# A windowed-attention and mixture-of-experts layer on one core: the first layer's projections in plain fp32 on 64-row tiles, and new pattern and attention stages

## The chip, the core and the metric

The kernel runs on one NeuronCore of a Trainium2 chip, one launch. The metric is the device time of that core in microseconds, median of the runs shown. It is written in Bass: every engine (TensorE or PE, VectorE or DVE, ScalarE or ACT, GpSimdE or POOL, SyncE or SP for the DMAs) has its own instruction stream, and they are tied together by semaphores by hand.

## What is computed

x is (2, 32, 32, 64), fp32: 2048 tokens of 64 channels, in 32 windows of 8 x 8. The first layer is an attention-like mixer with 8 heads of 32, the second a top-2 mixture of 8 experts.

```python
t = layernorm(x) @ W_prep + b_prep              # 64 -> 5 kinds x 8 heads x 32: q_n, q, k, k_m, v
bias, pat_n, pat_m = spatial(intrinsic)         # relative tables, 15 x 15 offsets
score  = bias + einsum('bhod,ohid->bohi', q_n, pat_n)      # pattern of the query's place
score += einsum('bhod,bhid->bohi', q, k)
score += einsum('bhid,ohid->bohi', k_m, pat_m)             # pattern of the key's place
score  = (score - mean_i) / sqrt(var_i(score) + 1e-5)      # no softmax
x = x + (einsum('bohi,bhid->bohd', score, v)) @ W_fin + b_fin
# second layer, on xt = layernorm(x)
logits = xt @ Wr + br;  two best experts, weights from their probabilities
y_e = gelu((layernorm(xt) * ln_g[e] + ln_b[e]) @ W1[e] + b1[e]) @ W2[e] + b2[e]
x = x + sum of the two chosen y_e, weighted
```

## The kernel before

Everything is kept in SBUF. The work is in four stages; TensorE's order is written out by hand: the early part line by line, `stage_b` (L70) gives the order of the pattern stage, and `pe_steps(t)` (L101) that of attention and FFN, one list for each step t. `make_plan` turns these lists into the fill and drain counts of the eight PSUM banks, and `begin`, `end`, `filled` and `drained` wait and count by them.

**Projections (L524 to L605).** DVE and ACT normalise x twice side by side into XN (token by channel), PE transposes it (L532) into PSUM, and `XS` gets the upper 64 partitions rounded to F32R (ACT, L846) and in the lower 64 the rest (DVE, L1038). W_prep lies twice under itself in `WS`; ACT and POOL split it into `WHI` and `WLO` (L836, L848, L434). `project` (L551) multiplies all 128 rows of XS by WHI and by WLO, two F32R matmuls, and so gets nearly fp32. `prep` (L557) makes the two query kinds and the key pattern kind in chunks c = 0 to 5 of four banks each, `keys` (L547) makes K. `shift_bias` (L514) folds ln_b into the experts' first bias: 16 matmuls with one column each, half ahead of the first projections and half behind the second chunk, from W1E, loaded for it. `centred` (L536) makes the windows' centred values XC. ACT and DVE take the results out of PSUM: `stage` (L796) into `STG`, KT at L863 and L1053, XC at L867 and L1058. SP then copies STG by DMA into `BD` (L368), a buffer that holds for every head only its own 32 rows, the others zero, so that one matmul with all 128 rows keeps four heads apart. There are two BD buffers of 1024 columns for six chunks.

**Pattern stage (`pattern`, L568).** 32 tiles of one bank; in each, for four places u and two head groups g, a matmul of a slice of the tables PN or PM (128 rows, 64 columns) with 128 columns of BD, into the upper or lower half of the bank. For c < 2 ACT and DVE copy each tile into `TN` (`move_tn`, L810); for c >= 2 DVE adds the bias table BI and writes `TM` (L1085). POOL builds PM (L446), ACT builds PN (L858), DVE the bias rows EB (L1062), which go to DRAM and back.

**Attention (t = 0 to 16).** One window pair in each step: `score` (L620) puts four transposes of TM (L634) and four matmuls of KT with the zero-padded BD (L641) on top of each other in one bank, `values` (L615) makes V in two F32R matmuls (L617, L618), DVE adds TN into `SR` (L1144), ACT squares it (L932) and copies V into `BV` (L926), `weighted` (L645) makes the unnormalised output (L653), ACT copies it to OR (L940). Every four pairs: column sums of the squares (`ss`, L663), transposed (`st`, L715), the variance on DVE (L1098, L1105), its inverse root on POOL (L481), the scaling into ON on DVE (L1162), two transposes (`on`, L724), the last projection (`y`, L735), the sum into XR (L1178), the second norm with POOL's two small roots (L491, L496), the transpose `x2` (L753), split into X2 high and low again (L893, L1199), and the router `lg` (L746, with the split WRR). The steps at which these happen are the lags in `late`. ACT and DVE build the split first expert weights W1H and W1L from W1R (`weight_steps`).

**FFN (t = 16 to 33).** In each step u two experts for 512 tokens: `hidden` (L667), eight F32R matmuls into banks 0 to 3, Gelu on ACT (L887), `down` (L678) in plain fp32 on two column tiles, gating and adding on DVE (L1120, L1125). The gates go through DRAM and come back spread over the partitions (SP, L390, L397).

The names `B` and `X` in the profile are names with their numbers left out (B1, B2; X2).

## Time and profile before

| | us |
|---|---|
| median of 3 runs | 205.78 (205.74 to 208.18) |
| the profiled execution | 206.78 |
| its span, first to last instruction | 204.9 |
| PE busy | 187.5 (92%) |
| DVE, ACT, POOL busy | 121.8, 124.5, 58.9 |

The span is the part of the profiled execution from the first to the last instruction. PE's matmuls are pipelined, each lasts longer than its distance to the next one; the chain of waits gives the distances. "PEld" is the loading of the stationary operand. The idle time of an engine that isn't the bottleneck costs nothing.

### The profile page before, as it was taken

The numbers are of one execution on the slowest core, as the hardware profiler recorded it, in microseconds if no ns is written. First come the engines' busy times: TensorE is split into PE (matmuls) and PEld (weight loads), VectorE is DVE, ScalarE is ACT, GpSimd is POOL, SyncE is SP. The second block draws the span as 40 slices with busy tenths as digits, with TensorE's granted clock in tenths as the row PEclk, the third lists the DMA queues.
The fourth block names the chain that finished last, engine by engine and source line by source line (L and its number), as shares of the span: only waits on it lengthen the run. The fifth ranks groups of instructions, "written<-read, shape, count | busy, mean of one in ns | idle before, by whom it ended". The sixth has DMA issues, their size and how long they took to land.

```text
span 204.9 us, 4295 instructions
## 1 busy us (share of the span) xinstructions
PE 187.5 (92%) x1592; PEld 130.8 (64%) x1592; DVE 121.8 (59%) x335; ACT 124.5 (61%) x253; POOL 58.9 (29%) x86
## 2 busy tenths in 40 slices
PE   0089999999999999999999998999999999999993
PEld 0069789899898866666576685556655655554441
DVE  7991557995664722212543866736793776496353
ACT  6953587989614066666784786565456556666440
POOL 7927900000000120019075683609260006000000
PEclk9999999999999999999999999999999999999998
DMA  5960297028547290003003000140024001500610
GB/s 143 230 180 0 41 226 146 14 47 183 97 111 153 55 198 10 0 3 102 3 0 109 3 3 0 54 154 0 3 65 143 2 0 34 204 0 4 199 57 26
DMA packets 8740, 15.38 MB, mean 75 GB/s; under 512 B 3008, under 2 KB 4552, under 8 KB 8656
## 3 DMA queue, kind: packets, MB, share of 16 engines
q1 hardware_dynamic: 8656, 15.11, 29.2%
q8 instruction: 12, 0.20, 0.4%
q0 software_dynamic: 64, 0.01, 0.1%
q14 instruction: 8, 0.07, 0.1%
HBM read 8.20 MB, written 0.62 MB: 43 GB/s over the span
## 4 chain that ended last, share of the span: by engine, by line
PE 78%; DVE 10%; DMA 6%; ACT 2%; issue 2%; SPq 1%; DVEq 0%; ACTq 0%
PE PS L582 14%; PE PS L686 10%; PE PS L641 8%; PE PS L653 5%; PE PS L554 5%; PE PS L674 5%; PE PS L634 4%; PE PS L675 4%; PE PS L555 4%; PE PS L735 4%; DMA GB<-gate_rows 3%; PE PS L518 3%; PE PS L617 2%; DMA gate_rows<-GT 2%; PE PS L724 2%
## 5 line engine op out<-in xcount | busy, mean ns | idle before, releaser
L887 ACT ACTIVATE HR<-PS,B1P 128x512 f32<-128x512 f32 x64 | 38.8, 691 | 18.5 <-PE PS L675 18.1
L686 PE MATMUL PS<-HR,W2s 128*64 128x512 f32 x128 | 30.8, 604 | 0.0
L674 PE MATMUL PS<-X,W1H 128*128 128x512 f32 x64 | 26.6, 415 | 0.0
L1144 DVE TENSOR_TENSOR SR<-PS,TN 128x512 f32<-128x512 f32 x16 | 11.1, 691 | 25.9 <-PE PS L641 23.6
L675 PE MATMUL PS<-X,W1L 128*128 128x512 f32 x64 | 25.1, 393 | 0.0
L926 ACT ACTIVATE BV<-PS 64x256 f32<-64x256 f32 x32 | 12.3, 383 | 19.4 <-PE PS L618 14.0
L481 POOL TENSOR_TENSOR RSC<-VB,NHALF 128x32 f32<-128x32 f32 x4 | 21.8, 5460 | 0.3
L825 ACT ACTIVATE STG<-PS,BP 128x512 f32<-128x512 f32 x20 | 12.4, 689 | 14.1 <-PE PS L555 14.0
L641 PE MATMUL PS<-BD,KT 128*64 128x256 f32 x128 | 17.3, 392 | 0.0
L686 PEld LDWEIGHTS PS<-HR,W2s 128*64 128x64 f32 x128 | 7.8, 136 | 13.7 <-issue 12.8
L816 DVE COPY TN<-PS 64x256 f32<-64x256 f32 x32 | 13.7, 427 | 2.7 <-PE PS L582 2.1
L1085 DVE TENSOR_TENSOR TM<-PS,BI 128x512 f32<-128x512 f32 x16 | 11.1, 692 | 7.0 <-PE PS L582 6.9
L674 PEld LDWEIGHTS PS<-X,W1H 128*128 128x128 f32 x64 | 12.1, 189 | 4.5 <-issue 1.6
L465 POOL MEMSET BV<- 128x528 f32 x3 | 1.6, 543 | 45.5 <-PE PS L582 45.4
L582 PE MATMUL PS<-BD,PN 128*64 128x128 f32 x256 | 14.6, 274 | 0.0
L582 PE MATMUL PS<-BD,PM 128*64 128x128 f32 x256 | 14.6, 273 | 0.0
L554 PE MATMUL PS<-XS,WHI 128*128 128x512 f32 x32 | 14.5, 453 | 0.0
L582 PEld LDWEIGHTS PS<-BD,PN 128*64 128x64 f32 x256 | 13.9, 137 | 0.9 <-issue 0.7
L582 PEld LDWEIGHTS PS<-BD,PM 128*64 128x64 f32 x256 | 14.0, 137 | 0.7 <-issue 0.7
L532 PE MATMUL PS<-IDN,XN 128*128 128x128 f32 x16 | 4.1, 429 | 10.9 <-DVE XN L1030 10.9
L555 PE MATMUL PS<-XS,WLO 128*128 128x512 f32 x32 | 13.8, 431 | 0.0
L675 PEld LDWEIGHTS PS<-X,W1L 128*128 128x128 f32 x64 | 12.1, 188 | 2.1
(137 smaller groups left out, 334.2 us busy)
## 6 DMA issues: line engine op xcount, KB each, us to landing
BD<-STG SPq DMA_DIRECT2D x24, 256.0 KB, 4.8
GB<-gate_rows SPq DMA_DIRECT2D x32, 128.0 KB, 2.9
W1R<-in_W SPq DMA_DIRECT2D x4, 256.0 KB, 4.2
WS<-in_W_prep SPq DMA_DIRECT2D x2, 320.0 KB, 4.6
XR<-in_x SPq DMA_DIRECT2D x4, 128.0 KB, 2.5
W1E<-in_W SPq DMA_DIRECT2D x1, 512.0 KB, 6.7
W2s<-in_W SPq DMA_DIRECT2D x1, 512.0 KB, 3.6
out<-XR SPq DMA_DIRECT2D x4, 128.0 KB, 2.4
```

Source lines behind the costliest of these rows:

```text
L481: G.tensor_tensor(RSC[:, :, :, :].rearrange("p q h g -> p (q h g)"), vb, NHALF[:, :], ALU.pow).then_inc(rsc_ready, 1)
L554: nc.tensor.matmul(ps[:, :], WHI[:, col:col + P], moving, start=True, stop=False)
L555: return nc.tensor.matmul(ps[:, :], WLO[:, col:col + P], moving, start=False, stop=True)
L582: m = nc.tensor.matmul(ps[g * C:g * C + C, u * P:u * P + P], rows, moving, start=True, stop=True)
L641: m = nc.tensor.matmul(dst, KT[:, g, lo:lo + WT], slot[:, g, :, lq:lq + WT], start=False, stop=True, skip_group_check=True)
L674: nc.tensor.matmul(ps[:, :], W1H[:, col:col + P], X2[:, j * 512:j * 512 + 512], start=True, stop=False)
L675: end(nc.tensor.matmul(ps[:, :], W1L[:, col:col + P], X2[:, j * 512:j * 512 + 512], start=False, stop=True), "h", n)
L686: m = nc.tensor.matmul(ps[d * C:d * C + C, :], W2s[:, 2 * (2 * ep + d) + c, :], HR[(4 * u + 2 * c + d) % 8][:, :], start=(c == 0), stop=(c ...
L816: last = copy(TN[w * C:w * C + C, :, :, g, o0:o0 + 4].rearrange("p t h o -> p h t o"), src)
L825: return A(dst, src, ACT.Identity, bias=bias)
L887: A(HR[n % 8][:, :], PS[b][:, :], ACT.Gelu, bias=B1P[:, col:col + 1]).then_inc(bank_drained[b], 1)
L926: last = A(BV[tv % 3][w * C:w * C + C, :, w, 0:HD], PS[6][w * C:w * C + C, 0:256].rearrange("p (h d) -> p h d", h=NH), ACT.Copy)
```

## The change

All projections are plain fp32 matmuls on 64 rows of the array, one head group on the upper and one on the lower half, and so are the experts' first matmuls and the router: WHI, WLO, the split of XS and X2, W1H, W1L and WRR go. BD becomes four buffers `[P, 2, 2, 1024]`, only for the pattern kinds; each holds two heads in every 64 rows. The pattern stage works in 16 units of two banks on four quadrants of 64 x 64. Q isn't moved any more: `stage` writes it to QP, and `scores` multiplies 32 rows a head. Attention takes two window pairs in a round, with the heads' scores in banks 0 to 3. The bias shift moves to the first attention step; the inverse root of the variance moves from POOL to DVE, the EB copies from DVE to POOL; W1 is loaded whole after tile 15, DVE scales it in one pass into W1G. The steps of the rarer work are in a table.

```diff
+AT = {"ss": (4, 8, 12, 16), "st": (4, 8, 12, 18), "on": (8, 12, 18, 22), "y": (10, 14, 19, 23),
+      "x2": (12, 18, 22, 26), "lg": (14, 19, 23, 27), "out": (21, 25, 29, 33),
+      "spread": (4, 8, 12, 18), "scale": (7, 11, 17, 21), "x1": (10, 14, 20, 24),
+      "norm": (12, 17, 21, 25), "low": (13, 18, 22, 26), "route": (15, 19, 23, 27)}
 def stage_b():
-    for c in range(4):
-        for tile, numbers in ((True, range(2)), (False, range(4)), (True, range(2, 8))):
+    order = units(0, [0]) + chunk(2) + units(0, [1, 2, 3]) + chunk(3) + units(1, range(4))
+    order += units(2, [0]) + chunk(4) + units(2, [1, 2, 3]) + units(3, [0]) + chunk(5) + units(3, [1, 2, 3])
 def pe_steps(t):
+    if t < NPAIR:
+        if t % 2:
+            return []
+        p = t // 2
+        s = [(("v", p), 6, 1), (("score", p), 0, 1)] + at("ss", 7) + at("on", 6, 0) + at("lg", 6) + at("y", 7)
+        if p:
+            s += [(("o", p - 1), 4, 1)]
+        else:
+            s += [(("b1", c), 4 + c, 1) for c in range(2)]
+        return s + at("on", 6, 1) + at("st", 7) + at("x2", 6)
-        BD = [sb(f"BD{n}", [P, 2, 4, 1024]) for n in range(2)]
+        BD = [sb(f"BD{n}", [P, 2, 2, 1024]) for n in range(4)]
...
-            for c in range(6):
+            for c in range(4):
...
-                    sp.dma_start(BD[c % 2][r, :, h, :], STG[c % 2][r, :, :]).then_inc(bd_in[c % 2], 16)
+                    sp.dma_start(BD[c][r, :, h % 2, :], STG[c % 2][r, :, :]).then_inc(bd_in[c % 2], 16)
...
             def project(ps, kind, g, moving):
-                nc.tensor.matmul(ps[:, :], WHI[:, col:col + P], moving, start=True, stop=False)
-                return nc.tensor.matmul(ps[:, :], WLO[:, col:col + P], moving, start=False, stop=True)
+                return nc.tensor.matmul(ps[:, :], WS[g * C:g * C + C, col:col + P], moving, start=True, stop=True)
...
+            def pattern(unit):
+                for u in range(8):
+                    local = 8 * i + u
                     for g in range(2):
+                        for r in range(2):
+                            k = slice(r * C, r * C + C)
+                            rows = table[k, g, fx, WH - 1 - fy:2 * WH - 1 - fy, :].rearrange("p a b -> p (a b)")
+                            last[r] = nc.tensor.matmul(ps[r][g * C:g * C + C, u * C:u * C + C], rows,
+                                                       BD[c][k, g, :, 32 * local:32 * local + 32],
+                                                       start=True, stop=True)
...
-            pe.wait_ge(w1e_in, 16)
-            pe.wait_ge(lnb_in, 16)
-            shift_bias(range(4))
-            pe.wait_ge(whi_ready, 1)
-            pe.wait_ge(wlo_ready, 1)
+            pe.wait_ge(wprep_in, 32)
...
+            def scores(p):
...
+                begin("score", p)
+                for k in range(2):
+                    for h in range(4):
+                        lo = h * NW + 2 * (2 * p + k)
+                        nc.tensor.matmul(PS[h][:, k * P:k * P + P], TM[:, lo:lo + 2, :].rearrange("p w i -> p (w i)"),
+                                         IDN[:, :], start=(k == 0), stop=False, is_transpose=True,
+                                         skip_group_check=True)
+                for k in range(2):
                     for g in range(2):
+                        for w in range(2):
...
+                            for h in range(4):
+                                r = slice(HD * h, HD * h + HD)
+                                m = nc.tensor.matmul(PS[h][w * C:w * C + C, cols], KT[r, g, lo:lo + WT],
+                                                     QP[r, g, lo:lo + WT], start=False, stop=True,
+                                                     skip_group_check=True)
...
             def hidden(n):
-                c, d = divmod(r, 2)
+                d, c = divmod(r, 2)
+                k = slice(c * C, c * C + C)
-                nc.tensor.matmul(ps[:, :], W1H[:, col:col + P], X2[:, j * 512:j * 512 + 512], start=True, stop=False)
-                end(nc.tensor.matmul(ps[:, :], W1L[:, col:col + P], X2[:, j * 512:j * 512 + 512],
-                                     start=False, stop=True), "h", n)
+                end(nc.tensor.matmul(ps[:, :], W1G[k, 2 * ep + d, :], X2[k, j * 512:j * 512 + 512],
+                                     start=True, stop=True), "h", n)
...
@@ ACT, pattern stage @@
                 if not tile:
-                    stage(act, act_spread, c + 2, i)
+                    if c >= 4 or i % 2 == 0:
+                        stage(act, act_spread, c, i)
...
@@ DVE, pattern stage @@
                 if not is_tile:
+                    if c < 4 and i % 2:
+                        stage(dve, dve_spread, c, i)
                     continue
...
@@ DVE, variance @@
+                    step(V_.tensor_scalar(flat(VB), flat(VB), 0.0, 1.0 / (WT - 1), ALU.max, ALU.mult))
+                    step(V_.tensor_scalar(flat(VB), flat(VB), EPS_S, None, ALU.add))
...
+                    inverse_root(flat(RSC), flat(VB), flat(VA))
```

On DVE, in a round, the two additions into SR of the round (512 columns each, from banks 0 to 3 at once) stand in the queue ahead of that step's variance, and the normalised z (`centred`) ahead of them. ACT's order in a round: V's four copies, then the column sums and half of ON where they are due, two squares, the last round's two output copies, the other half of ON.

## Rows read from the trace of the kernel before

**Rows 1.** The page: the chain that ended last, shares by line

```profile
PE PS L582 14%; PE PS L686 10%; PE PS L641 8%; PE PS L653 5%; PE PS L554 5%; PE PS L674 5%; PE PS L634 4%; PE PS L675 4%; PE PS L555 4%; PE PS L735 4%; DMA GB<-gate_rows 3%; PE PS L518 3%; PE PS L617 2%; DMA gate_rows<-GT 2%; PE PS L724 2%
```

**Rows 2.** Windows by stage: length, then each engine's busy time

```profile
core 0: us, PE busy (x) PEld busy (x) DVE busy (x) ACT busy (x) POOL busy (x), PEclk, DMA share, GB/s
...
15.04:33.78 18.74, 18.74 (x98) 16.38 (x100) 8.97 (x14) 10.96 (x21) 8.46 (x19) 1.00 0.50 108
33.78:52.24 18.46, 18.46 (x274) 16.77 (x274) 15.55 (x42) 16.88 (x41) 0.00 (x0) 1.00 0.36 73
52.24:71.50 19.26, 18.96 (x278) 17.00 (x274) 12.24 (x19) 5.71 (x11) 0.60 (x2) 1.00 0.51 111
71.50:124.38 52.88, 52.75 (x570) 35.82 (x571) 22.90 (x62) 35.41 (x83) 23.31 (x24) 1.00 0.17 42
124.38:204.90 80.52, 74.48 (x368) 41.69 (x364) 49.54 (x143) 44.85 (x85) 16.48 (x25) 0.99 0.18 60
```

**Rows 3.** The chain in order of time: start, its length, line, instructions

```profile
15.01 3.50 PE PS L518 x16
...
22.23 0.43 PE PS L554
...
23.52 0.24 PE PS L554
...
24.47 1.87 PE PS L518 x16
...
30.21 3.57 PE PS L542 x32
...
37.77 7.14 PE PS L582 x128
...
78.82 0.59 PE PS L634 x4
79.41 1.01 PE PS L641 x8
80.42 0.32 PE PS L617
...
80.86 0.62 PE PS L653 x16
...
86.78 1.00 PE PS L663 x8
...
106.67 1.93 PE PS L735 x16
...
129.21 0.24 PE PS L674
...
130.60 1.87 PE PS L686 x8
```

**Rows 4.** Timeline of ACT: start, length, line, tile, idle before

```profile
24.62 2.48 ACT L858 ACTIVATE PN<-REL 128x240 f32<-128x240 f32 x8
...
78.30 0.78 ACT L926 ACTIVATE BV<-PS 64x256 f32<-64x256 f32 x2 [0.81 <-PE PS L618]
79.10 0.63 ACT L932 ACTIVATE SQ<-SR 128x512 f32<-128x512 f32 x1
79.76 0.39 ACT L940 ACTIVATE OR<-PS 128x264 f32<-128x264 f32 x1
```

**Rows 5.** Timeline of DVE

```profile
8.55 0.18 DVE L996 SCALAR_TENSOR_TENSOR RA<-RS 128x16 f32<-128x16 f32 x1
8.76 0.17 DVE L997 TENSOR_TENSOR RA<-RA,VE 128x16 f32<-128x16 f32 x1
...
37.08 8.95 DVE L816 COPY TN<-PS 64x256 f32<-64x256 f32 x20
...
70.81 0.69 DVE L1085 TENSOR_TENSOR TM<-PS,BI 128x512 f32<-128x512 f32 x1 [0.18 <-PE PS L582]
...
73.37 0.69 DVE L1144 TENSOR_TENSOR SR<-PS,TN 128x512 f32<-128x512 f32 x1 [1.87 <-PE PS L641]
```

**Rows 6.** Timeline of POOL: the inverse root of 32 columns

```profile
92.32 5.47 POOL L481 TENSOR_TENSOR RSC<-VB,NHALF 128x32 f32<-128x32 f32 x1
```

More of the change, by code:

```diff
@@ L70, in stage_b @@
 def stage_b():
-    order = []
-    for c in range(4):
-        for tile, numbers in ((True, range(2)), (False, range(4)), (True, range(2, 8))):
-            order += [(tile, c, i) for i in numbers]
+    units = lambda c, numbers: [(True, c, i) for i in numbers]
+    chunk = lambda c: [(False, c, n) for n in range(4)]
+    order = units(0, [0]) + chunk(2) + units(0, [1, 2, 3]) + chunk(3) + units(1, range(4))
+    order += units(2, [0]) + chunk(4) + units(2, [1, 2, 3]) + units(3, [0]) + chunk(5) + units(3, [1, 2, 3])
     return order
 def make_plan():
-    plan = [(("b1",), 3, 1)] + [(("xt", j), (0, 1, 2, 7)[j], 1) for j in range(NG)]
+    plan = [(("xt", j), (0, 1, 2, 7)[j], 1) for j in range(NG)]
     def prep(c, n):
@@ L591, in _ @@
+                for r in range(2):
+                    end(last[r], "t", 2 * unit + r)
+            pe.wait_ge(wprep_in, 32)
             for n in range(4):
-                if n < 2:
-                    pe.wait_ge(*drained("xt", 2 * n))
-                    pe.wait_ge(*drained("xt", 2 * n + 1))
+                if n % 2 == 0:
+                    pe.wait_ge(*drained("xt", n))
+                    pe.wait_ge(*drained("xt", n + 1))
                 prep(0, n)
@@ new lines, in weighted @@
+            def weighted(p):
+                if p == 0:
+                    pe.wait_ge(bv_zeroed, 4)
+                    pe.wait_ge(*drained("b1", 1))
+                pe.wait_ge(*drained("score", p))
+                pe.wait_ge(*drained("v", p))
+                begin("o", p)
+                for k in range(2):
+                    t = 2 * p + k
+                    for h in range(4):
+                        for g in range(2):
+                            m = nc.tensor.matmul(PS[4 + k][g * C:g * C + C, h * 66:h * 66 + 66],
+                                                 SR[t % 4][:, (2 * h + g) * C:(2 * h + g) * C + C],
+                                                 BV[t % 4][:, 4 * g + h, :, :].rearrange("p w d -> p (w d)"),
+                                                 start=True, stop=True)
+                end(m, "o", p)
@@ new lines, in output_transposed @@
+            def output_transposed(j, half):
+                act.wait_ge(*filled("on", j, half))
+                b = before[("on", j, half)][0]
+                if half == 0 and j >= 1:
+                    act.wait_ge(*filled("y", j - 1))
+                for q in range(2):
+                    src = PS[b][:, 2 * q * P:2 * q * P + 2 * P].rearrange("p (w g o) -> p g w o", w=2, g=2)
+                    last = A(ONT[:, 2 * half + q, :, :].rearrange("p g (w o) -> p g w o", w=2), src, ACT.Copy)
+                last.then_inc(bank_drained[b], 1)
@@ new lines, in rows @@
+            def rows(p):
+                for a in (2 * p, 2 * p + 1):
+                    if a >= 8:
+                        act.wait_ge(on_ready, a - 7)
+                if p == 0:
+                    act.wait_ge(*filled("bd", 5, 3))
+                act.wait_ge(*filled("o", p))
+                q0 = (2 * p) % 8
+                for k in range(2):
+                    last = A(OR[:, q0 + k, :, :, :].rearrange("p h w d -> p (h w d)"), PS[4 + k][:, 0:264], ACT.Copy)
+                last.then_inc(bank_drained[4], 1)
@@ L973, in _ @@
                 if t >= LAG:
-                    output_transposed(t)
+                    for j in due("ss", t):
+                        column_sums(j)
+                    for j in due("on", t):
+                        for half in range(2):
+                            output_transposed(j, half)
                     router_tanh(t)
@@ L1125, in _ @@
                         V_.tensor_tensor(AC[j % 2][:, :], AC[j % 2][:, :], GM[:, :], ALU.add).then_inc(gate_done, 1)
-                j, r = divmod(t - LAG - 6, 4)
-                if r == 0 and 0 <= j < NG:
+                for j in [j for j in range(NG) if AT["out"][j] == t - 1]:
                     y = XR[:, 4 * j:4 * j + 4, :]
```

570 lines of the change are left out of this document (248 added, 322 removed).

## The prediction

> **What bounds the kernel now.** I read the chain of waits first. All its large shares are lines of TensorE, the pattern matmuls' 14% first; the largest other one is a DMA with 3% [rows 1]. Then the five stages from 15.0 us on in windows: TensorE is busy all but 0.4 us from 15.0 to 124.4, and idle 6.0 of the 80.5 us after that; ACT and DVE stand close to it in one place, the first half of the pattern stage, with 16.9 and 15.6 of 18.5 us [rows 2]. So what TensorE spends per step is the time, and the question is which engine comes next. For the size of a step I read the same chain in order of time [rows 3]: it gives the spacing of matmuls, not their latency.
>
> **Prices on TensorE.** A matmul in plain fp32 is issued as two instructions (64 calls of L641 are 128 records), one in F32R as one. Full-height fp32 on two column tiles, 512 columns: 8 instructions in 1.87 us, 0.234 us each, against 0.24 for one F32R of 512 columns on the whole array. So one fp32 instruction streams at half speed (0.43 us for 512 columns) and two column tiles run side by side. L663 uses four 32-column tiles: 8 instructions of 512 columns in 1.00 us, that is two steps of 0.43 and some 0.14 us for changing over, which every block pays. The pattern's 128 instructions of 128 columns on two tiles take 7.14 us, 0.056 each [rows 3]. No row shows two *row* tiles (64 of the 128 rows each) at work together; all of the change rests on that. The bounds for a matmul on 64 rows: full overlap (half the price) and none. I take full overlap, since the column tiles show it and the halves touch other rows and other banks. The Trainium skill ("TensorEngine Tiling (Array Packing)", Key Properties) says that tiles load and multiply independently, and that a change of tiling mode drains the engine; the 0.14 us agree with the second.
>
> **1. Start (15.0 to 30.2 us before).** The bias shift's first half, 3.50 us at the low clock (its neighbours, fp32r of 512 columns, come every 0.43 us until 22.9 and every 0.24 after), and its second half (16 more, 1.87 us) leave this stage [rows 3]. (The granted clock reads 1.00 there too; by the spacing it is 1.2 GHz until 22.9 and 2.4 after.) XS is a plain copy by ACT and DVE, two each; all four are drained by about 15.9, so the first projections start at 15.05 instead of 18.5. Eight projections are four pairs of 4 instructions: 1.72 us a pair at the low clock (twice two times 0.43), 0.94 at the high one. Before, the level rose 4.4 us after the first projection; the same gives 19.5, so 2.6 pairs cold and 1.4 warm: done at 20.8, not 24.4. But the gain isn't kept whole: ACT's last staging copy ends at 21.8, then PN takes 2.48 us [rows 4], and keys 4 to 7 need banks that ACT frees only after PN: from 25.1. The keys end near 26.9, so the centring starts at 27.0 instead of 30.2: 3.2 us. Bounds: 1.9 us gained if all eight are cold, 4.5 if ACT were no limit.
>
> **2. Pattern stage (33.8 to 71.5).** Instructions double (1024), each of 64 columns on four quadrants: 0.056 x 1/2 (columns) x 1/2 (twice the tiles) = 0.014 us, so a unit of 64 costs 0.9 us and 16 units 14.3 against 28.6. Each half has 8 units and two chunks of four projections (8 instructions, 1.87 us): 11 us of TensorE. In the first half DVE is next: 32 TN copies, 20 in 8.95 us [rows 5], make 14.3 us, and four staging copies come to it, 3.0: 17.3 us. (ACT hands four of its eight stagings over and has some 14 us left of its 16.9.) They began at 37.08 [rows 5], 6.9 us behind the centring at 30.2 [rows 3]; of that 1.5 were the EB copies, which go to POOL, idle there: so the centring + 5.4, 32.4, and the end at 49.7. In the second half it has 16 TM additions of 0.69 [rows 5], 11.1 us; TensorE needs 12, and a chunk of 1.9 us between two units starves DVE twice, 1.6 us in all. Attention so starts at 62.4 instead of 71.5: 9.1 us gained, 3.2 of them from part 1. The moves of BD (now four buffers, two chunks fewer) land by some 42 and 49 us, before they are asked for. The W1 load (after tile 15) and BV's clearing by POOL go into this stage too, where nothing waits for them.
>
> **3. Attention (71.5 to 124.4).** Two window pairs share a round. Per round: values 4 F32R of 256 columns, 0.65; 8 transposes, 1.02; QP against KT on 32-row by 64-column tiles, 64 instructions of 64 columns, eight side by side: 8 x 0.056 + 0.14 = 0.6, where two pairs cost 2.0; weighting 32 instructions 1.09. Sum 3.36 us against 5.3 (two of 0.59 + 1.01 + 0.44 + 0.62) [rows 3]; eight rounds 26.9. Beside them lie three column sums 3.0, their transposes 1.8, two ON 2.1, two y 3.9, x2 and the router 1.5, and the bias shift 1.9 (32 loads of 0.117, halved): 41.1 us. ACT has per pair 0.80 + 0.66 + 0.39 [rows 4], 3.7 a round, 29.6 and 5 more: it fits, with little room. The inverse root moves from POOL, 5.5 us each [rows 6], to DVE, where it is 12 steps 0.21 apart [rows 5], 2.5 us in DVE's own queue: the next round's SR additions stand behind it, the bank group of the scores is freed late, about 1 us three times; the ON copies share a bank with the next values, another 1 us in all. Some 45 us, 7.8 gained. W1H and W1L (3.7 us of ACT and 3.5 of DVE) go, W1G costs DVE one pass of about 1.2; both were covered.
>
> **4. FFN (124.4 to 203).** `hidden` is 8 fp32 instructions, paired, 1.87 us per step against 8 F32R and a start, 1.99: 0.12 x 16 = 1.9 us. The down projection, Gelu (2.4 of some 3.9 us per step) and the gates are unchanged.
>
> Sum: 9.1 + 7.8 + 1.9 = 18.8 us. The profiled execution took 206.78 (span 204.9), so 188.0; the median of the runs is 1.0 us below it: 187.
>
> **Rivals.**
> *A, issue.* 1024 and 512 instructions each with a weight load must be handed out every 14 and 7 ns. The trace shows no such rate over a long stretch: 16 in 0.62 us, some 29 ns after the changeover, is the densest. At 28 ns a unit costs 1.8 us; the second half of the pattern stage becomes 8 x 1.8 + 3.7 + 1 = 19.1 us instead of 12.7, the first 0.8 more, the scores 1.3 more in each round (10.8, of which 4 fill the stalls of part 3): 14 us back, 201. For it: nothing denser is shown. Against: neither of those stretches was short of anything but its own streaming. The Trainium skill ("TensorE: Matmul & The Clock Gate", Wait — 56ns, not 53.3ns?) has start to start never under about 25 ns; if that held for the engine and not for each tile, the same sum would give 197. The rule speaks against this change.
> *B, the other side.* If instructions come no faster than the one long stretch that I can read, 0.056 us each, the pattern costs 57 instead of 28.6 us and the scores 28.6 instead of 16.2: 41 us lost, 10 gained elsewhere, 237. It decides from about 35 ns on. The 29 ns of the weighting speak against it, over 16 only.
> *C, the halves don't overlap.* Projections and `hidden` double (15 and 30 us more) and the pattern gains nothing: about 245. The four column tiles speak against it.
> *D, attention keeps its pace.* ACT, DVE and TensorE hand each other one group of banks; if each round waits for a full turn, attention stays near 52 us and only the start and the pattern gain: 195.
>
> **How the numbers follow.** Forecast 0.55, with its own range 181 to 194 (cold start 1.3, DVE's stalls 2, attention 4 either way); D 0.13; A 0.20; B 0.06, C 0.03, 0.03 for better still. The range 180 to 201 takes in D and most of A. This kernel's measurement tells about 2% from no change; 2% below 205.8 is 201.7: faster 0.84, within 2% 0.06, slower 0.10.
>
> **What would show it.** TensorE's first projection near 15.1 and a gap before key 4; the pattern's units 0.9 us long with TensorE idle between them and DVE's TN copies back to back; the first transposes near 62; rounds of 4 to 5.5 us with 0.6 for the scores; `hidden` near 1.87 per step. Units of 1.6 us or more with TensorE full say A; 3.6, B; `hidden` at 3.6, C. If DVE's copies aren't back to back in the first half, step 2 is wrong; if rounds last longer than 5.5 us though the scores take 0.6, step 3.

## The result, and the profile after

The changed kernel takes 201.59 us, median of 4 runs (199.29 to 204.11), beside 205.76 us (203.90 to 208.18) of the kernel before. Each kernel's executions fall into a faster and a slower group, and the ratio compares the faster ones alone: 0.970 (95% interval 0.962 to 0.977), 3.0% faster; the two medians would give 0.980. A second series of six executions, made later, gave 201.32 us and a ratio of 0.977 (0.966 to 0.989). The forecast of 187 was 14.6 us too low and its range (180 to 201) just misses the median. The profiled execution took 199.29 us, its span is 197.5 us where the forecast's own sum makes 186.1 (204.9 less 18.8): 11.4 us are to be explained. The rest of the 14.6 is no matter of the stages: the profiled execution is 2.3 us under the median of the four, and the forecast had taken 1.0 us off its own profiled one.

The page's chain that ended last, shares by line. `hidden` (L662) and `down` (L673) now lead it; the pattern's matmuls (L560 here, L582 before) have fallen from 14% [rows 1] to 4%, and 8% of the span is "issue", time in which the engine waited for nothing that the profile shows.

```profile
PE 59%; DVE 18%; ACT 10%; issue 8%; DMA 2%; POOL 1%; SPq 1%; ACTq 0%; DVEq 0%; POOLq 0%
```

Windows by stage (length, then each engine's busy time, PEclk, DMA share, GB/s): projections and keys, first half of the pattern stage with the centring, second half, attention, FFN. They answer to [rows 2].

```profile
16.97:28.53 11.56, 9.55 (x34) 3.86 (x33) 5.95 (x8) 6.96 (x15) 2.58 (x6) 1.00 0.47 105
28.53:51.11 22.58, 16.44 (x554) 13.13 (x553) 18.63 (x38) 16.47 (x38) 0.00 (x0) 1.00 0.63 137
51.11:69.66 18.55, 15.41 (x539) 11.12 (x540) 11.73 (x20) 7.47 (x15) 3.03 (x12) 0.91 0.17 39
69.66:115.96 46.30, 41.72 (x988) 35.32 (x988) 28.17 (x99) 29.07 (x72) 4.55 (x10) 1.00 0.02 4
115.96:197.50 81.54, 75.14 (x379) 30.42 (x376) 48.21 (x143) 45.46 (x86) 8.98 (x19) 1.00 0.18 60
```

Stage by stage against the forecast: the centring starts at 28.53 (forecast 27.0, before 30.2), attention at 69.66 (62.4, before 71.5), the FFN at 115.96 (107.4, before 124.4). So 1.5 us are missing at the start, 5.7 in the pattern stage, 1.3 in attention (46.3 for 45) and 2.9 in the FFN (81.5 for 78.6). The pattern stage is half of the miss: from centring to attention it takes 41.1 us, as long as before (41.3), though its matmuls cost half.

That they cost half is plain in TensorE's timeline (start, length, line, tile, idle before and what ended it):

```profile
44.52 0.34 PE L560 MATMUL PSUM<-BD,PN 64*64 64x64 f32 x6 [0.25 <-issue]
46.01 1.16 PE L560 MATMUL PSUM<-BD,PN 64*64 64x64 f32 x64 [1.15 <-DVE TN L814]
47.80 1.05 PE L560 MATMUL PSUM<-BD,PN 64*64 64x64 f32 x57 [0.63 <-DVE TN L814]
51.11 0.34 PE L560 MATMUL PSUM<-BD,PN 64*64 64x64 f32 x7 [2.26 <-issue]
51.35 1.39 PE L560 MATMUL PSUM<-BD,PM 64*64 64x64 f32 x64
52.67 3.39 PE L532 MATMUL PSUM<-XS,WS 64*128 64x512 f32 x8
55.99 2.10 PE L560 MATMUL PSUM<-BD,PM 64*64 64x64 f32 x128
58.63 0.92 PE L560 MATMUL PSUM<-BD,PM 64*64 64x64 f32 x46 [0.55 <-DVE TM L1081]
```

A unit of 64 instructions lasts 1.1 to 1.2 us; two without a wait between them take 2.10 us, 16 ns an instruction. Four quadrants do work side by side. But in the midst of unit (1,3), behind its 57th instruction, TensorE stands still for 2.26 us with no semaphore to wait for, and right behind that everything is slower: chunk 4's eight projections take 3.39 us, where eight others take 1.99. The windows show why (same columns as above):

```profile
45.00:50.00 5.00, 2.21 (x121) 2.00 (x121) 4.26 (x10) 2.99 (x8) 0.00 (x0) 1.00 1.01 239
50.00:55.00 5.00, 3.89 (x77) 2.62 (x79) 2.99 (x6) 1.67 (x5) 1.30 (x4) 0.71 0.77 179
55.00:60.00 5.00, 4.00 (x178) 2.77 (x175) 2.48 (x4) 2.37 (x4) 1.73 (x8) 0.95 0.06 11
```

While TensorE pauses, all 16 DMA engines are full (share 1.01, 239 GB/s): these are the moves of chunks 2 and 3. Then the granted clock goes from 2.4 to 1.2 GHz for a while (PEclk 0.71 and 0.95 in the next two windows). The page's list of DMA queues has a row that I hadn't read before. Of the kernel before:

```profile
q8 instruction: 12, 0.20, 0.4%
```

and of the changed one:

```profile
q8 instruction: 20, 0.33, 0.7%
```

These are packets of instructions, 16 KB each (0.33 MB by 20), and there are two thirds more of them. From the timeline above the period can be counted: pauses ahead of the sixth-last instruction of unit (1,1) and ahead of the seventh-last of (1,3), 6 + 64 + 57 = 127 matmuls apart, with as many weight loads: some 256 records. The totals agree: the page counts 2504 matmuls and as many loads, 19.6 times 256, for the 20 packets, and 1592 of each, 12.4 times 256, for the 12 of the kernel before.

### The profile page after: what moved, and what is told of

Same layout as the page of the kernel before. It is cut to its first block, busy times and chain, and to the rows that moved or that the text cites. A ratio compares the mean times of both kernels' runs of the same rounds, so it can differ in the third digit from the quotient of the medians.

```text
span 197.5 us, 6111 instructions
## 1 busy us (share of the span) xinstructions
PE 162.4 (82%) x2504; PEld 96.9 (49%) x2504; DVE 125.8 (64%) x365; ACT 115.2 (58%) x236; POOL 34.5 (17%) x82
## 4 chain that ended last, share of the span: by engine, by line
PE 59%; DVE 18%; ACT 10%; issue 8%; DMA 2%; POOL 1%; SPq 1%; ACTq 0%; DVEq 0%; POOLq 0%
PE PSUM L662 12%; PE PSUM L673 11%; PE PSUM L532 7%; DVE TN L814 5%; PE PSUM L560 4%; PE PSUM L725 4%; ACT HR L883 3%; PE PSUM L613 3%; PE PSUM L623 3%; PE PSUM L640 2%; DVE XN L1034 2%; PE PSUM L520 2%; DVE TM L1081 2%; DMA XR<-in_x 2%; PE PSUM L651 2%
## 5 line engine op out<-in xcount | busy, mean ns | idle before, releaser
L883 ACT ACTIVATE HR<-PSUM,B1P 128x512 f32<-128x512 f32 x64 | 38.8, 688 | 22.2 <-PE PSUM L662 22.2
L662 PE MATMUL PSUM<-X,W1G 64*128 64x512 f32 x128 | 31.8, 615 | 0.0
L673 PE MATMUL PSUM<-HR,W2s 128*64 128x512 f32 x128 | 30.8, 604 | 0.0
L532 PE MATMUL PSUM<-XS,WS 64*128 64x512 f32 x64 | 19.0, 732 | 2.0 <-ACT KT L858 2.0
L662 PEld LDWEIGHTS PSUM<-X,W1G 64*128 64x128 f32 x128 | 11.0, 186 | 11.7 <-issue 11.0
L673 PEld LDWEIGHTS PSUM<-HR,W2s 128*64 128x64 f32 x128 | 7.9, 136 | 17.7 <-issue 16.8
L939 ACT ACTIVATE BV<-PSUM 64x256 f32<-64x256 f32 x32 | 12.2, 383 | 6.0 <-PE PSUM L593 5.8
L814 DVE COPY TN<-PSUM 64x256 f32<-64x256 f32 x32 | 13.6, 426 | 2.7 <-PE PSUM L560 2.0
L1172 DVE TENSOR_TENSOR SR<-PSUM,TN 128x512 f32<-128x512 f32 x16 | 10.3, 686 | 7.9 <-PE PSUM L623 7.8
L871 ACT ACTIVATE TN<-PSUM 64x256 f32<-64x256 f32 x32 | 12.1, 377 | 5.2 <-PE PSUM L560 4.7
L560 PE MATMUL PSUM<-BD,PN 64*64 64x64 f32 x512 | 9.4, 221 | 6.1 <-DVE TN L814 3.6
L1081 DVE TENSOR_TENSOR TM<-PSUM,BI 128x512 f32<-128x512 f32 x16 | 10.0, 684 | 5.9 <-PE PSUM L560 5.9
L560 PEld LDWEIGHTS PSUM<-BD,PN 64*64 64x64 f32 x512 | 8.4, 135 | 8.4 <-issue 8.3
L560 PE MATMUL PSUM<-BD,PM 64*64 64x64 f32 x512 | 9.4, 223 | 2.1 <-DVE TM L1081 1.1
L560 PEld LDWEIGHTS PSUM<-BD,PM 64*64 64x64 f32 x512 | 8.5, 137 | 4.4 <-issue 3.1
```

Source lines behind the costliest of these rows:

```text
L532: return nc.tensor.matmul(ps[:, :], WS[g * C:g * C + C, col:col + P], moving, start=True, stop=True)
L560: last[r] = nc.tensor.matmul(ps[r][g * C:g * C + C, u * C:u * C + C], rows, BD[c][k, g, :, 32 * local:32 * local + 32], start=True, stop=True)
L662: end(nc.tensor.matmul(ps[:, :], W1G[k, 2 * ep + d, :], X2[k, j * 512:j * 512 + 512], start=True, stop=True), "h", n)
L673: m = nc.tensor.matmul(ps[d * C:d * C + C, :], W2s[:, 2 * (2 * ep + d) + c, :], HR[(4 * u + 2 * d + c) % 8][:, :], start=(c == 0), stop=(c ...
L814: last = copy(dst, src)
L871: move_tn(act, lambda dst, src: A(dst, src, ACT.Copy), 8 * c + 2 * i + r, 0)
```

## The experiments

Theory S (supply), after seeing this: TensorE's instructions come through the same DMA engines as the data, in blocks; where a block is used up faster than the next arrives, it pauses, and a running transfer makes the block late. All runs but one are the changed kernel with an edit; the small move, half the instructions and `hidden` whole leave work out or change values and are there for their timing alone. "Pauses" is the sum of the causeless idle times in the midst of units in the one profiled execution; "attention" is its first transposes.

| run | median us (n) | pause in unit (1,3) | all pauses | centring | attention | clock of the profiled execution |
|---|---|---|---|---|---|---|
| changed kernel | 201.59 (4) | 2.26 | 3.5 | 28.5 | 69.7 | 0.991 |
| the same again | 201.32 (6) | 2.10 | 3.1 | 26.1 | 68.3 | 0.957 |
| small move | 199.66 (4) | 0.61 | 1.3 | 25.8 | 63.4 | 0.991 |
| spaced moves | 200.39 (5) | 3.08 | 4.6 | 27.7 | 70.5 | 0.962 |
| PN early | 198.60 (4) | 3.08 | 6.2 | 24.3 | 67.0 | 0.953 |
| POOL late | 198.56 (4) | 2.53 | 6.2 | 26.1 | 69.1 | 0.980 |
| bias from POOL | 200.96 (4) | 2.81 | 4.8 | 27.9 | 69.4 | 0.983 |
| three combined | 196.94 (6) | 2.03 | 5.9 | 22.5 | 66.7 | 0.953 |
| half the instructions | 196.41 (3) | none | 0 | 25.9 | 62.9 | 0.974 |
| `hidden` whole | 200.32 (3) | 2.65 | 4.2 | 28.1 | 71.2 | 0.965 |
| chunk 3 late | 198.20 (6) | none | 4.7 | 27.2 | 68.1 | 0.991 |
| four combined | 196.80 (6) | 0.34 | 4.8 | 23.7 | 65.2 | 0.969 |
| four, W1 later | 196.70 (6) | 0.61 | 5.0 | 24.4 | 64.7 | 0.965 |

The kernel before, in the same four series, each on a chip of its own: 209.00 us (small move to POOL late), 206.71 (bias from POOL to `hidden` whole), 207.17 (chunk 3 late and four combined) and 207.13 (four with W1 later, and the same again). Executions of these variants differ by 3 to 7 us among themselves, mostly with the granted clock (the section on the hardware), so a median of four tells 1 us from another only poorly. What tells the theories apart are the places and lengths of the pauses.

**1. A small move.**

```diff
-                    sp.dma_start(BD[c][r, :, h % 2, :], STG[c % 2][r, :, :]).then_inc(bd_in[c % 2], 16)
+                    cols = slice(0, 64 if c == 3 else 1024)
+                    sp.dma_start(BD[c][r, :, h % 2, cols], STG[c % 2][r, :, cols]).then_inc(bd_in[c % 2], 16)
```

> The third pair of zero-padded moves (chunk 3) carries 64 of its 1024 columns, so 15/16 of that transfer is left out, and the part of the scores that rests on it with it. Theory S (supply): TensorE's 2.26 us without a cause at 48.9 us is its instructions coming late, because they are fetched over the same DMA engines that two overlapping moves fill; the clock's fall at 52 us follows from the pause. Expected: no gap over 0.6 us between 45 and 53 us, granted clock 1.00 in 50:60, chunk 4's eight matmuls 1.99 us instead of 3.39, first transposes of attention near 66 instead of 69.7, span 3 to 4.5 us shorter. Rival N (instruction count): the pause comes at a fixed place of the instruction stream whatever the DMA queues carry; then the gap stays at 1.5 us or more and the time within 1 us. Rival T (thermal or power throttle by density): the gap goes and the clock falls all the same, gain 2.3 us.

TensorE's timeline at the same two places:

```profile
45.11 1.05 PE L561 MATMUL PSUM<-BD,PN 64*64 64x64 f32 x57 [0.64 <-DVE TN L815]
46.77 0.34 PE L561 MATMUL PSUM<-BD,PN 64*64 64x64 f32 x7 [0.61 <-issue]
```

The pause stays at the same instruction and shrinks from 2.26 to 0.61 us; the clock holds through 60 us, and from the centring to attention it takes 37.6 us instead of 41.1. Both halves of S: the place belongs to the instruction stream (N is right so far), the length to the DMA traffic. The clock fell later, at 68 us, so the span's 192.8 isn't all the edit's. Attention starts 6.2 us earlier than in the changed kernel, 2.7 of them by an earlier start of the centring.

**2. Half the instructions.** The other side of S: the traffic stays, the stream is halved.

```diff
-                for u in range(8):
+                for u in range(0, 8, 2):
...
-                            last[r] = nc.tensor.matmul(ps[r][g * C:g * C + C, u * C:u * C + C], rows,
-                                                       BD[c][k, g, :, 32 * local:32 * local + 32],
+                            last[r] = nc.tensor.matmul(ps[r][g * C:g * C + C, u * C:u * C + 2 * C], rows,
+                                                       BD[c][k, g, :, 32 * local:32 * local + 64],
```

> The pattern stage issues half of its matmuls, each with twice the columns: the same columns streamed, half the instructions; the odd places get the table slice of their neighbour, so the pattern's values there are others. Theory S (instructions come in blocks over the DMA engines): the causeless pauses in the midst of units (0.25, 2.26, 0.55, 0.40 in the changed kernel) are gone or under 0.3 us, and a unit takes 0.9 instead of 1.1 us; attention's first transposes 4 to 5 us earlier, near 65. Rival D (DMA traffic hinders TensorE's operands themselves, or the pauses are the clock's doing): pauses stay at their times, near 49 us.

The stretch from 44 us, TensorE:

```profile
44.24 1.10 PE L560 MATMUL PSUM<-BD,PN 64*64 64x128 f32 x32 [1.09 <-DVE TN L814]
46.05 1.10 PE L560 MATMUL PSUM<-BD,PN 64*64 64x128 f32 x32 [0.70 <-DVE TN L814]
47.84 1.10 PE L560 MATMUL PSUM<-BD,PM 64*64 64x128 f32 x32 [0.70 <-DVE TN L814]
48.88 1.99 PE L532 MATMUL PSUM<-XS,WS 64*128 64x512 f32 x8
50.80 1.98 PE L560 MATMUL PSUM<-BD,PM 64*64 64x128 f32 x64
53.39 2.30 PE L560 MATMUL PSUM<-BD,PM 64*64 64x128 f32 x64 [0.61 <-DVE TM L1081]
```

Every pause is gone, with the DMA share at 0.84 between 45 and 50 us, and the page counts 16 packets of instructions, four fewer, for 1992 matmuls (15.6 times 256 records). What is left are the waits for DVE that the forecast had named. This expectation's rival D is false. Attention starts at 62.9, 36.9 us behind the centring; the forecast had 35.4, and chunk 3 alone took 1.6 us more than the other chunks here, at 1.2 GHz (3.57 for 1.99). So the forecast's pattern stage was right for a TensorE that always has its next instruction. One miss: a unit still takes 1.10 us, so it was not the instruction count that made it 1.1 instead of 0.9.

**3. Moving the traffic.** Three edits: spacing chunk 3's moves; issuing the bias rows and their 16 loads from POOL's queue (the same lines with `pool` for `sp`, behind EB's copies), so that SP is free for chunk 2's moves earlier; and holding chunk 3's moves until unit (1,3) is done, with the W1 load behind tile 21.

```diff
+                    if c == 3 and h:
+                        sp.wait_ge(*filled("t", 7 + 2 * h))
```

> Nothing is left out. Chunk 3's four moves are issued one at a time, behind pattern tiles 9, 11 and 13, instead of together. Theory S: the queues are never full for long, the gap at 48.9 shrinks to under 1 us and the clock holds at 1.00 through 60 us: 2 to 4 us faster, unless the last of the four lands too late for unit (3,1) (the moves are first read behind unit 7, near 50 us), in which case a wait on the move stands in the gap's place. Rival N: gap unchanged, time within 1 us.

> Nothing is left out: the bias rows and their 16 loads are issued from POOL, which idles from 20 to 52 us, so that SP is free for chunk 2's moves from about 36.5 us instead of 41. Theory S: what prolongs TensorE's pause is the transfer of chunks 2 and 3 at the same time; with chunk 2's moves 4 to 5 us earlier, and the first three runs' lesson that the pause always lies behind the 57th matmul of unit (1,3), the pause falls from 2.3 to 3.1 us to about 1 us (chunk 3's moves alone still run then) and the clock doesn't fall at 52: 2 to 3 us faster. Rival N2: the pause is that long because chunk 2's moves, whenever they run, delay some block of instructions: then a pause of 2 us or more stands at an earlier place of the instruction stream, and the time stays within 1 us.

```diff
+                if c == 3:
+                    sp.wait_ge(*filled("t", 15))
...
-            sp.wait_ge(*filled("t", 15))
+            sp.wait_ge(*filled("t", 21))
```

> Nothing is left out. Chunk 3's four moves wait for the end of unit (1,3) (tile 15), and the W1 load for tile 21; the rest is the changed kernel. Theory S in its sharper form, from the runs so far: TensorE's instructions come in blocks of 256, the next one is asked for when the last is entered, and takes 2.4 us from there with the DMA queues quiet and 4.1 to 4.9 with a move running; two pattern units in a row use one up in 1.8 us. The crossing that hurts lies at 46.5 to 48.9 us, when chunk 2's move ends and chunk 3's runs. With chunk 3's move behind it the pause should be 0.6 to 1.2 us instead of 2.3 to 3.1, and 1 to 2.5 us come off the span (chunk 2's move runs to about 46 and may still cover part of it). If a new pause of over 1 us appears behind tile 15 or at unit (3,0) instead, the traffic was only shifted.

Spacing didn't help (pause 3.08 us): chunk 2's move and the first of chunk 3's already cover the crossing from one block to the next. With the bias rows on POOL chunk 2's move was over by 43 us (the window from 43 to 44 has a DMA share of 0.08), but chunk 3's then ran alone from 44.5 to 49.6 and the pause was 2.81, with the clock's fall behind it as before: the expectation of 1 us missed, and with it the thought that two moves at once are needed. One is enough. Holding chunk 3's moves does remove this pause, and the others show the rule best (TensorE, chunk 3 late):

```profile
45.26 1.29 PE L562 MATMUL PSUM<-BD,PN 64*64 64x64 f32 x70 [2.33 <-issue]
47.55 1.99 PE L562 MATMUL PSUM<-BD,PN 64*64 64x64 f32 x64 [1.00 <-DVE TN L816]
49.35 1.78 PE L562 MATMUL PSUM<-BD,PM 64*64 64x64 f32 x64
...
55.63 0.92 PE L562 MATMUL PSUM<-BD,PM 64*64 64x64 f32 x46 [0.55 <-DVE TM L1083]
58.27 1.44 PE L562 MATMUL PSUM<-BD,PM 64*64 64x64 f32 x82 [1.72 <-issue]
```

None at (1,3), but 2.33 us at the crossing before it, which now lies under chunk 2's move, and 1.72 at the one in unit (2,3), under the later moves, where the changed kernel has 0.55. "The traffic was only shifted" is what the expectation called this case. My sharper form of S was half right. The period is 127 matmuls, so two units and not one: a block lasts some 3.6 us at DVE's pace in the first half, not 1.8. In the changed kernel the block entered at 44.5 is followed by the next at 51.1, 6.6 us later, under full queues (7.0 in its second profile). With the queues at rest it went from 56.7 to 60.1 and from 64.0 to 67.2 (the timeline's places of the 127th matmuls): 3.3 to 3.4 us, with pauses of 0.55 and 0.40 in them. Here the one entered at 45.3 is used up 3.8 us later, at rest, and no pause follows; the clock, at 1.2 GHz from 47.4 us on, gave it part of that time (in the four combined, at the high clock, 0.34 us are left).

The trace also keeps when each packet of instructions ran. In the twelve profiles with the full stream there are 46 pauses at a crossing in the pattern stage, and TensorE goes on 1.2 to 1.6 us after the end of a 16 KB packet in every one of them (in the changed kernel at (1,3): packet from 48.31 to 49.64, TensorE at 51.11). The packet itself takes 0.9 to 1.4 us. What the moves change is its start: 0.6 to 1.8 us after the last block was entered with the queues at rest (24 pauses, DMA share under 0.3), 1.3 to 4.7 us with them full (19 pauses, share over 0.8; 3.79 at (1,3)). Of the other three, one had a share of 0.75 and two are the first crossing. From entry to entry this makes 3.0 to 4.6 us at rest and 3.6 to 7.5 us with a move running. So S is not only inferred from where the pauses stand: the late packet is there to see.

**4. Earlier starts.** PN built on ACT behind the two XS copies instead of ahead of the keys; POOL behind DVE's normalisation; and combinations.

```diff
@@ ACT, in the loop over the XS copies @@
+                act.wait_ge(reln_in, 16)
+                for oj in range(2 * j, 2 * j + 4):
+                    src = REL[:, 0, :, ::-1].rearrange("p g (y c) -> p g y c", c=SIDE)
+                    last = A(PN[:, :, oj, :, :], src[:, :, :, WH - 1 - oj:2 * WH - 1 - oj], ACT.Copy)
```

> ACT builds the query table PN in two halves behind its two XS copies instead of behind its last query staging. My step 1 says that keys 4 to 7 wait for ACT only because PN (2.48 us) stands ahead of its key copies: expected PE's 2.0 us gap before 26.5 goes, centring starts near 26.7 instead of 28.5, and the span is 1.5 to 2 us shorter if the staging copies aren't held up (they need bank 0 at 18.8, ACT would be done with PN near 19.5, so up to 0.7 us comes back). Rival: the first pattern half is set by DVE's 32 TN copies and DVE is itself still busy at that point, so the gain is swallowed: centring earlier but the first TN copy not, time within 0.5 us.

```diff
+            pool.wait_ge(xn_ready, NDVE)
             step(pool.memset(CEN[:, :], 0.0))
```

> POOL waits for DVE's normalised tiles before it builds CEN and PM. Theory H (shared port): DVE's XN operations take 446 ns instead of 381 because POOL now works beside them; without that they go back to about 380, 12 x 65 ns = 0.8 us, the transposes end near 16.2 instead of 17.0 and everything behind is 0.8 us earlier (0.4% of the time). PM would be done near 18 us, long before its first use at 55. Rival: the longer XN is the input's or the semaphore's doing: XN stays at 446 ns and nothing moves.

PN early: the 2.0 us gap ahead of key 4 is gone and the centring starts at 24.3, 1.8 us before that of an execution with the same start (26.1). POOL late: DVE's 12 normalisations, in the changed kernel and then here (DVE's timeline):

```profile
10.45 4.50 DVE L1034 SCALAR_TENSOR_TENSOR XN<-XR,MV,RS 128x128 f32<-128x128 f32 x12
```

```profile
11.34 3.23 DVE L1035 SCALAR_TENSOR_TENSOR XN<-XR,MV,RS 128x128 f32<-128x128 f32 x12
```

3.23 us instead of 4.50 (in the other profiles that leave POOL's place alone 4.08 or 4.09 seven times and 4.31 once, 3.23 in the three combinations that move it): beside POOL's copies of PM they are 26 to 39% longer. The Trainium skill ("SBUF — State Buffer", Who interferes with whom) says that a DVE instruction with two SBUF inputs contends with a GpSimd instruction that reads SBUF; the durations agree. In this execution the input also came late (XN from 11.34), so that the transposes ended at 16.5; in the run of the three combined, with XN from 9.60, they ended at 14.8, 0.8 us earlier than in its neighbours (15.6).

> Three edits together, nothing left out: bias rows issued from POOL, PN built early on ACT, POOL behind DVE's normalisation. If they add up: 2.5 + 1.5 + 0.7, some 4 us less than the changed kernel, 194 to 196 us. If the first half of the pattern stage is limited by the blocks of instructions and not by where it starts, only the earlier start (about 2) is left: 198.

> The combination of four edits, nothing left out: the three of the combined run (bias rows from POOL, PN early, POOL behind DVE's normalisation) and chunk 3's moves behind tile 15, the W1 load behind tile 21. The combined run had its fast ones at 195.1 to 197.3 with a pause of 2.0 us left at unit (1,3). Theory S: the pause falls to 0.6 us and the clock has no reason there to fall: 193 to 195 us, clock above 0.975 in most runs. Rival: the clock falls anyway, at another place, and the time stays at 196 to 197.

> As the four edits together, but the W1 load waits for tile 25 (unit (3,0)) instead of 21. In that run it was issued at 50.2 us, just before the crossing in unit (2,3), and a pause of 2.53 us stood there. Theory S: that pause falls to 0.3 to 0.6 us, and none over 1 us takes its place except possibly at the crossing in the last three units (W1's transfer then runs about 60 to 64 us): 1.5 us or more off the span, 190 to 195 us by the clock of the run. Rival: W1 landing later holds up the bias shift in the first attention round, and the gain is given back there.

The combinations join the edits above: bias from POOL, PN early and POOL late; the same with chunk 3 late and W1 behind tile 21; and with W1 behind tile 25. They start the centring at 22.5 to 24.4, 1.7 to 3.6 us before the 26.1 of the changed kernel's second profile, and end at medians of 196.7 to 196.9 us, 4.5 us under the changed kernel and 5% under the kernel before (four, W1 later: ratio 0.951, interval 0.940 to 0.963, beside 0.977 of the changed kernel on the same chip; best single execution of the four combined 191.56). They beat both kernels. The three combined lie between the two outcomes that their expectation named (194 to 196, or 198); for the four its rival came true, the clock fell all the same, at 54 us, and the time stayed at 196 to 197. The pauses did not fall in sum (5.9, 4.8 and 5.0 us, 3.5 and 3.1 in the changed kernel): shifting moved them from one crossing to another, 1.41 and 2.53 us in the four combined, 1.78, 1.38 and 1.22 with W1 later. With the shifts added the median moved by 0.1 to 0.2 us only, which speaks for the earlier start as the source of the gain; that is not shown cleanly, since chunk 3 late alone, with the centring where it was, had 198.2. The expectation that the pause at (2,3) would fall to 0.3 to 0.6 us missed: 1.38. Chunk 3's moves were issued until 50.0 us and still filled the queues there.

**5. `hidden` on the whole array.**

```diff
-                end(nc.tensor.matmul(ps[:, :], W1G[k, 2 * ep + d, :], X2[k, j * 512:j * 512 + 512],
-                                     start=True, stop=True), "h", n)
+                nc.tensor.matmul(ps[:, :], W1G[:, 2 * ep + d, :], X2[:, j * 512:j * 512 + 512],
+                                 start=True, stop=False)
+                end(nc.tensor.matmul(ps[:, :], W1G[:, 2 * ep + d, :], X2[:, j * 512:j * 512 + 512],
+                                     start=False, stop=True), "h", n)
```

> The experts' first matmul is made on the whole array in F32R, twice with the same weights, as the kernel before did with its two halves of the weight: 8 instructions of 512 columns for 8, values not the layer's, all else the same. My step 4 gave row tiles 0.12 us a step. Theory C (change-over): the row-tiled form itself is 1.92 against 1.99 to 2.03, but every small whole-array block beside it now pays about 0.17 us more (gates' transpose, x2, y, out), so the two forms come out equal: FFN stage 81 to 82 us in both, each small block 0.15 to 0.2 us shorter here. Rival: FFN's extra is the clock or the gates' waits, and the small blocks cost the same in both; then this form is 2 us slower than the changed kernel's.

Of the changed kernel and of this one, the same two blocks of the FFN, the gates' transpose and `out`:

```profile
159.68 1.94 PE L673 MATMUL PSUM<-HR,W2s 128*64 128x512 f32 x8
161.77 0.29 PE L754 MATMUL PSUM<-IDN,PG 128*32 128x128 f32 x1 [0.15 <-DVE PG L1205]
161.99 1.99 PE L662 MATMUL PSUM<-X,W1G 64*128 64x512 f32 x8
163.90 1.94 PE L673 MATMUL PSUM<-HR,W2s 128*64 128x512 f32 x8
165.77 0.66 PE L775 MATMUL PSUM<-IDN,AC 128*128 128x128 f32 x4
166.36 1.99 PE L662 MATMUL PSUM<-X,W1G 64*128 64x512 f32 x8
```

```profile
144.68 0.28 PE L756 MATMUL PSUM<-IDN,PG 128*32 128x128 f32 x1
144.72 0.48 PE L662 MATMUL PSUM<-X,W1G 128*128 128x512 f32 x1
...
148.59 0.66 PE L777 MATMUL PSUM<-IDN,AC 128*128 128x128 f32 x4
149.00 0.48 PE L662 MATMUL PSUM<-X,W1G 128*128 128x512 f32 x1
```

From the gates' transpose to `hidden` 0.22 against 0.04 us, from `out` 0.59 against 0.41. Eleven steps, from the `down` that starts at 138.97 to the one at 189.15, take 50.18 us in the changed kernel and 49.18 here (142.81 to 191.99): a step without anything between is 0.11 us shorter with row tiles (3.79 against 3.90), one with `out` alone 0.09 longer, a step with the gates 0.30 longer, one with ON 0.44. Theory C holds for the small blocks: 0.18 us each. But the change-over only cancels the gain. Of the 1.0 us, 0.9 is later starts of the gates' transposes (2.09 behind `down` instead of 1.87, three times) and a longer wait for DVE ahead of ON (0.48 instead of 0.24); why these come later with row tiles stays open. The rival, 2 us slower without row tiles, is false.

**6. The changed kernel again.**

> The changed kernel once more, beside the other one and the kernel before on one chip. No theory is at stake but the size of the effect: 199 to 204 us, 2.5 to 4% under the kernel before, its slower executions those with the lower granted clock (about 1.4 us for each 0.01 of clock); pause behind the 57th matmul of unit (1,3) 2 to 3 us again.

As expected: 201.32 us, a pause of 2.10 us behind the 57th matmul of unit (1,3). Here the input was on time, and the centring started at 26.1, with the clock's rise to 2.4 GHz at 17.3 us instead of 21.4.

## Why the prediction was wrong

**Prices on TensorE: right but for the scores.** All of the change rested on two row tiles working together, which no row had shown: they overlap fully. A projection chunk takes 1.92 to 1.99 us for 1.87, two units 2.10 for 1.8, the scores of two pairs 0.85 for 0.6 (64 instructions, from 70.72 to 71.57), the rest is the change-over and 0.2 us a unit. The scores' price was 0.25 us too low, 2.0 us in eight rounds. Rivals B and C are out.

**Part 1, start (1.5 us of the miss).** Its working was right: the clock rises 4.5 us after the first projection (16.90 to 21.40; the forecast took 4.4), and key 4 waits 2.0 us for ACT behind PN. What was off is the first projection itself, at 16.90 for 15.05. DVE's normalisation, costed as unchanged, became 0.8 us longer beside POOL's copies of PM (4.50 for 3.71): POOL had been waiting for WHI there (a wait of 4.9 us in the kernel before), and with WHI gone its copies moved ahead into DVE's time. The rest is the input of this execution: XN started at 10.45, before at 9.27, and in eight of the twelve others between 9.54 and 9.61 or, in four, between 10.49 and 11.60. With it on time the moment of the clock's rise decides: in chunk 3 late it came 4.5 us after the first projection again, and the centring started at 27.2, close to the forecast's 27.0; in the second profile of the changed kernel it came 1.7 us after, and the centring started at 26.1. No run shows what sets that moment.

**Part 2, pattern (5.7 us).** This is the step that failed: "a unit of 64 costs 0.9 us and 16 units 14.3". As a price for streaming it holds. It left out that 1024 instructions and their weight loads must first be brought. The pauses sum to 3.5 us, and the clock of 1.2 GHz between 52 and 55.5 us makes chunk 4 1.4 and unit (2,0) 0.3 us longer; the rest, 0.5, is what shows of the 0.2 us a unit. DVE tells the same story. Its TN copies began 5.5 us behind the centring (forecast 5.4) and ran back to back as forecast, but for one hole of 2.04 us, the pause:

```profile
51.50 1.76 DVE L814 COPY TN<-PSUM 64x256 f32<-64x256 f32 x4 [2.04 <-PE PSUM L560]
57.20 2.48 DVE L1081 TENSOR_TENSOR TM<-PSUM,BI 128x512 f32<-128x512 f32 x4 [2.62 <-PE PSUM L560]
```

The other 3.7 us are in the second half, where DVE stood idle for 5.9 us and the forecast had 1.6 (its additions took 10.0 us instead of 11.1); the longest of these waits, 2.62, is that for the slow chunk 4. The forecast had looked for the supply and named it as rival A with 0.2, 28 ns a matmul. For a burst A is wrong (16 ns). Over a whole block it is nearly what the chip gives: 127 matmuls in 3.4 us, as at the crossings at rest, are 27 ns. A's price was right, its reach was not: it binds only where two units stand close together, and there DVE or the projections take about as long, so that it showed as four pauses and not as 14 us. The forecast also called the moves of BD harmless since they land "before they are asked for". No matmul waited for them, indeed; their cost was that of the queues they filled.

**Part 3, attention (1.3 us).** Right in sum, 46.3 for 45, and in part by luck. TensorE was busy for 41.7 us (forecast 41.1) and idle for 4.6 (forecast 4). Most of the scores' 2.0 us too many was made up by blocks that came out below their price. Of the stalls, DVE's inverse root cost 1.26 us once, where three of about 1 us were expected, and ACT's copies 3.3 (0.79, 0.88, 0.69 and 0.94), where 1 was. The forecast's sign of rounds over 5.5 us came up too: from first transposes to first transposes a round takes 3.5 to 8.4 us, the long ones those with ON, y and x2 in them. The sign was badly set, since the forecast's own sum makes 5.6 on average.

```profile
87.27 1.07 PE L613 MATMUL PSUM<-IDN,TM 128*128 128x128 f32 x8 [1.26 <-DVE SR L1172]
...
93.66 0.39 PE L592 MATMUL PSUM<-WVH,XC 128*128 128x256 f32 x1 [0.79 <-ACT ONT L898]
```

Rival D is out.

**Part 4, FFN (2.9 us).** "0.12 x 16 = 1.9 us" is the term. The 0.11 us a step are there, but the small whole-array blocks between `down` and `hidden` had been free of a change-over on one side, `hidden` being whole too. Row-tiled, it makes each of them pay 0.18 us more, some 2 us for the twelve that stand ahead of a `hidden` (gates, `out`, x2, y): as much as the 1.8 that the row tiles save. The stage became 1.0 us longer than before; the fifth experiment points to later starts behind DVE for most of that. The forecast had counted 0.14 us for changes in the blocks that it rewrote and none in the neighbours that it didn't touch. The first gates also come later relative to TensorE (a wait of 1.59 us at the first transpose of the gates, 120.5; 0.98 before).

The total: 3.0% faster was on the right side, and the mechanisms named were there; what was missing was a resource that no line of the kernel names, and a cost that stands in lines the change leaves alone.

## What to carry to other kernels

Halving an instruction's work halves its time only while the instructions arrive: multiply the count of a dense stretch by the bytes of a record, see in the page's DMA list how many instruction blocks the kernel had before, and compare the pace of a block with what it took when the queues were full and at rest. Large transfers don't only need to land in time, they should not lie over a dense stretch of small matmuls; where there are several such stretches, shifting a transfer shifts the pause, and fewer, longer instructions are what helps. When a block's tiling mode changes, price the change-over at its neighbours too.

## What the hardware showed that was not expected

- Instructions of TensorE are fetched during the run, in blocks of 16 KB, through the DMA engines (20 packets, before 12). The next block is there 3.0 to 4.6 us after the last was entered with the queues at rest, 3.6 to 7.5 with a move running (46 pauses), and TensorE goes on 1.2 to 1.6 us after the packet's end. The pause that this makes has no releaser in the profile ("issue" in the midst of a group of equal instructions is its mark).
- Four quadrants of 64 x 64 take 16 ns an instruction, and 64 instructions on eight tiles of 32 x 64 take 0.85 us, 13 ns each. The Trainium skill ("TensorE: Matmul & The Clock Gate", Wait — 56ns, not 53.3ns?) has start to start never under about 25 ns; across tiles these rows are well under it.
- The granted clock. In all variants it falls to 1.2 GHz once or several times between 24 and 122 us, for 3.4 us or more (in the changed kernel at 52, with the small move at 68, with half the instructions at 37 and 106); often behind a pause, but with half the instructions, where there is none, too: there the first fall comes 0.9 us after TensorE had waited 2.0 us for DVE. Waits of the same length stand elsewhere without a fall (2.01 us ahead of key 4 in the changed kernel), and the falls at 106 to 115 us follow waits of 0.7 to 0.9 us that had ended 5 us and more before. So the pause isn't its only cause, and what is stays open. It counts: over the 61 executions of the thirteen rows of the table, each measured from its own kernel's mean, 0.01 of mean clock is 1.4 us (correlation -0.83). The kernel before shows no such tie in 42 executions (-0.25).
- DVE with two SBUF inputs: 0.27 us an instruction with POOL silent, 0.34 to 0.37 beside POOL's copies.
